# Cross-attention steps of a two-layer attention kernel: value products moved ahead of the next transposes, normalising moved ahead of the probabilities' split

## The reference, cut to what matters

```python
def attention(x, ctx, Wq, Wk, Wv, Wo, bo):
    q = (x @ Wq).reshape(b, n, HEADS, D_HEAD)
    k = (ctx @ Wk).reshape(b, m, HEADS, D_HEAD)
    v = (ctx @ Wv).reshape(b, m, HEADS, D_HEAD)
    sim = jnp.einsum('bihd,bjhd->bhij', q, k) * SCALE
    attn = jax.nn.softmax(sim, axis=-1)
    out = jnp.einsum('bhij,bjhd->bihd', attn, v).reshape(b, n, HEADS * D_HEAD)
    return out @ Wo + bo
h = layernorm(x, ln2_g, ln2_b)
x = attention(h, context, a2_Wq, a2_Wk, a2_Wv, a2_Wo, a2_bo) + x
```

## Time and profile before

| | before |
|---|---|
| median of 3 runs | 1027.96 us (1027.17 to 1029.55) |
| profiled execution, its time | 1026.68 us |
| its span | 1024.9 us |
| TensorE busy | 981.0 us, 96% |
| VectorE busy | 704.5 us, 69% |
| ScalarE busy | 624.1 us, 61% |
| GpSimd busy | 366.3 us, 36% |
| mean granted TensorE clock | 0.981 of 2.4 GHz |
| self-attention, by the trace | about 160 to 565 us |
| cross-attention | about 565 to 877 us |
| feed-forward | about 877 us to the end |

### The profile page before, as it was taken

One profiled execution on the slowest core, in us unless ns is written; L12 is line 12 of the kernel. 1 busy time (PEld: TensorE's weight loads), 2 busy tenths in 40 slices (PEclk: granted clock), 3 DMA queues, 4 the chain that ended last, 5 costly groups with the idle time before them and its releaser, 6 DMA issues.

```text
span 1024.9 us, 21429 instructions
## 1 busy us (share of the span) xinstructions
PE 981.0 (96%) x7892; PEld 921.9 (90%) x7892; DVE 704.5 (69%) x1594; ACT 624.1 (61%) x1945; POOL 366.3 (36%) x514
## 2 busy tenths in 40 slices
PE   7799999999999999999999999999999997999998
PEld 6687877899999999999999989999999997999998
DVE  5577578767676767676778777667667667566674
ACT  5556457757575756565667676676666667433343
POOL 1222337433333333342423345455454545301010
PEclk9799899999999999999999989999999999999999
DMA  7311100104000000000003000200000001001010
GB/s 219 102 42 42 36 21 32 32 2 104 2 22 1 23 1 22 2 21 2 22 2 88 21 27 23 87 27 27 2 27 26 2 22 62 22 22 38 26 32 22
DMA packets 30445, 34.62 MB, mean 34 GB/s; under 512 B 4360, under 2 KB 23816, under 8 KB 30344
## 3 DMA queue, kind: packets, MB, share of 16 engines
q1 hardware_dynamic: 30344, 33.26, 10.7%
HBM read 24.86 MB, written 8.39 MB: 32 GB/s over the span
## 4 chain that ended last, share of the span: by engine, by line
PE 81%; DVE 8%; ACT 7%; issue 2%; POOL 1%; SPq 0%; DMA 0%; DVEq 0%; ACTq 0%
PE bank L1386 15%; PE bank L1388 14%; PE bank L1387 14%; PE bank L1647 8%; PE bank L1626 5%; PE bank L1403 5%; PE bank L1689 3%; PE bank L1691 3%; PE bank L1690 3%; PE bank L1663 3%; ACT p L769 2%; PE bank L1508 1%; PE bank L1509 1%; PE bank L1510 1%; DVE hT_lo L1142 1%
## 5 line engine op out<-in xcount | busy, mean ns | idle before, releaser
L577 POOL TENSOR_TENSOR oT_hi<-oT,ones 128x256 fp32r<-128x256 f32 x128 | 93.9, 733 | 362.7 <-DVE oT L1182 362.7
L769 ACT ACTIVATE p<-bank,negmax 128x256 f32<-128x256 f32 (+1 forms) x512 | 207.8, 427 | 20.2 <-DVE negmax L1159 15.9
L779 ACT CAST pT_hi<-bank 128x512 fp32r<-128x512 f32 (+1 forms) x256 | 110.7, 486 | 166.6 <-PE bank L1647 166.4
L1386 PE MATMUL bank<-hT_hi,w_hi 128*128 128x256 f32 x640 | 188.5, 295 | 3.9 <-DVE qkT_lo L1213 1.6
L1388 PE MATMUL bank<-hT_hi,w_lo 128*128 128x256 f32 x640 | 179.0, 280 | 0.0
L1387 PE MATMUL bank<-hT_lo,w_hi 128*128 128x256 f32 x640 | 178.9, 280 | 0.0
L1174 DVE TENSOR_TENSOR pT_lo<-bank,pT_hi 128x512 fp32r<-128x512 f32 (+1 forms) x256 | 129.6, 547 | 0.5
L1155 DVE TENSOR_REDUCE negmax<-bank 128x2 f32<-128x512 f32 x128 | 82.1, 683 | 66.9 <-PE bank L1626 66.9
L1386 PEld LDWEIGHTS bank<-hT_hi,w_hi 128*128 128x128 f32 x640 | 121.6, 190 | 7.0 <-issue 3.6
L1387 PEld LDWEIGHTS bank<-hT_lo,w_hi 128*128 128x128 f32 x640 | 121.4, 190 | 0.0
L1388 PEld LDWEIGHTS bank<-hT_hi,w_lo 128*128 128x128 f32 x640 | 121.0, 189 | 0.0
(11 more groups left out here) (204 smaller groups left out, 2738.9 us busy)
## 6 DMA issues: line engine op xcount, KB each, us to landing
w_stage<-in_weights SPq DMA_DIRECT2D x47, 256.0 KB, 4.6
x_in<-x_dram SPq DMA_DIRECT2D x24, 256.0 KB, 2.9
x_dram<-x_out SPq DMA_DIRECT2D x16, 256.0 KB, 3.2
l_x<-in_x SPq DMA_DIRECT2D x4, 512.0 KB, 5.0
x_dram<-l_out SPq DMA_DIRECT2D x4, 512.0 KB, 2.8
out_dram<-x_out SPq DMA_DIRECT2D x8, 256.0 KB, 3.1
w_stage<-in_weights SPq DMA_DIRECT2D x9, 128.0 KB, 5.6
l_ctx<-in_ctx SPq DMA_DIRECT2D x4, 180.0 KB, 4.4
```

The source lines that it names most:

```text
L577: nc.gpsimd.tensor_tensor(oh[:, G % PAIRS, :], of[:, :], ones[:, :], ALU.mult).then_inc(y["o_hi"], 1)
L769: last = nc.scalar.activation(p[:, G % 2, e, t * cols:(t + 1) * cols], scores_at(G, e, t), ACT.Exp, bias=negmax[:, G % 2, t, e:e + 1], acc ...
L779: nc.scalar.copy(pTh[0:r, G % 2, e, 0:n], bank[4 + e][0:r, 0:n]).then_inc(y["pT_hi"], 1)
L1386: nc.tensor.matmul(dst, lh, rh, start=(i == 0), stop=False)
```

## The change

In the 64 steps of the cross-attention stage, and only there, three instructions or groups of instructions change their place within the step. TensorE issues the value products of the pair before right behind the scores of the next pair, ahead of this pair's transposes. ScalarE copies that pair's transposed sums ahead of rounding this pair's transposed probabilities. VectorE normalises that pair's output ahead of this pair's low part. What each instruction computes, its operands and its semaphores stay as they are.

```diff
@@ step_cross, ScalarE
                     round_values(b + 1, 0)
+                copy_rT(G - 1)
                 round_pT(G)
                 if G + 1 < STEPS:
                     softmax_pair(G + 1)
...
                     weights_hi(act, 17 + i)
-                copy_rT(G - 1)
@@ step_cross, VectorE
                     values_low(b + 1, 0)
+                normalise_o(G - 1)
                 pT_low(G)
                 if i == 0:
                     prepare_stats(b + 1)
...
                     weights_lo(dve, 17 + i)
-                normalise_o(G - 1)
@@ step_cross, TensorE
                 if G + 1 < STEPS:
                     scores(G + 1)
+                weighted_values(G - 1)
                 transpose_p(G)
...
                 if i in (5, 6) and more:
                     project_queries(b + 1, i - 5)
-                weighted_values(G - 1)
                 if i == 0:
                     project_out(b - 1, 3 if b == B else 5, 6)
```

## The result

The changed kernel takes 1040.62 us (median; 1039.53 to 1041.24) where the kernel before takes 1027.62 us. The ratio is 1.0122, 95% interval 1.0104 to 1.0139: slower by 13 us, as forecast. The profiled span went from 1024.9 to 1037.7 us, +12.8 us.

What follows compares the result with a forecast made beforehand. TensorE was taken as the bound, busy 343 of the stage's 360 us. Terms 3.7 + 0.6 - 2.0 + 10.4 = +12.7 us on 1026.7 give 1039.4; with 1.3 to the median, forecast 1040.5 us, range 1029 to 1051.

Steps and rivals of the forecast that it cites:

- part d: Step 4: key products (line 1403) wait for VectorE's context_low (line 1148) seven times, about 1.8 us, 3 in batch 8.
- The shift per ordinary batch: Key products start 0.61 us later in each ordinary batch, bounds 0.18 and 1.00; six batches give +3.7 us.
- nothing gives the 0.61 us back: After step 4's key products no further wait, order and distances as before, so the 0.61 us delay stays.
- `hT_lo`'s step of 0.82 us: On VectorE, from hT_lo to v_lo: 0.82 us, bounds 0.61 and 1.03, where it took 1.03 us before.
- 747.85 is 747.30 plus the operation's own time: Old trace, by the skill's exclusion rule: hT_lo ends its own duration after GpSimd's x_plus_bias ended.
- part g: TensorE's clock falls after the new 2.0 us idle time in four of six batches, 2.6 us each: +10.4 us.
- Batches 8 and 15: Batch 8, same chain with one weight unit: +0.6 us; batch 15, value products sooner: -2.0 us (bounds -2.9 and -1.2).
- Rival 1: TensorE's clock holds after the new idle time; only +2.3 us remain, 1030.3 us; chance 0.18.
- Rival 2: Clock falls in all six ordinary batches, as long as in batch 8: 20.4 us instead of 10.4, 1050.5 us; chance 0.12.
- Rival 3: context_low doesn't take the wait over, if step 3's chain moves by less than 0.75 us: 1015 us; chance 0.12.
- (c): VectorE's normalise_o ahead of pT_low: in step 3 it runs in idle time, taking 0.33 us off the chain.
- (a): TensorE's value products ahead of the transposes: free for TensorE, but dependent ScalarE and VectorE work starts 0.93 us later.

Runs made afterwards that it cites:

- after_late_lows: Changed kernel with VectorE's prepare_lo and values_low moved from step 3 to step 4, behind context_low: 1018.55 us, ratio 0.9899.
- old_in_34: Changed kernel with the old order on all three engines in steps 3 and 4 of each batch: 1024.51 us, ratio 0.9974.
- after_busy: Changed kernel with twelve transposes of the identity added on TensorE in step 4, behind pair 4's transposes: 1025.70 us, ratio 0.9968.
- late_all: after_late_lows with ScalarE's prepare and round_values also in step 4 and VectorE's weight-unit low parts one step later: 1008.53 us, ratio 0.981.
- before_late_all: Kernel before, without the change's three moves, with all the later moves of late_all: 1008.79 us, ratio 0.9812.
- pe_only: Kernel before with TensorE's move alone; ScalarE and VectorE keep their old order: 1083.87 us, ratio 1.054.
- norm_late: Changed kernel with VectorE's normalise_o put back at the end of its step: 1085.32 us, ratio 1.0552.
- no_pe_move: Changed kernel with TensorE's move taken back, ScalarE's and VectorE's moves kept: 1135.92 us, ratio 1.1059.

## Why the prediction was right, point by point

**The new wait** (what is late next, part d). Right: line 1403 on VectorE's line 1148, seven times, 1.65 to 1.68 us in ordinary batches (forecast about 1.8) and 2.93 in batch 8 (forecast 3). Its cause is shown by `after_late_lows`, its place by `old_in_34`.

**The shift per ordinary batch** was mis-sized: 0.33 us by `after_busy`, where I had 0.61 (within the bounds 0.18 and 1.00). Two things are at fault. `copy_rT` was costed at 0.22 us ahead of the rounding; the rounding moved by 0.98 us, of which 0.93 are the value products, so the copy costs 0.05: it runs beside the transposes and is nearly hidden by them. And "nothing gives the 0.61 us back" was not quite true: the key products come 0.42 us later against the context transposes, but a batch is only 0.33 longer. The other 0.1 us comes back somewhere in the six other steps; I haven't pinned it down, but it is of the size of the 0.15 us by which `late_all`'s ordinary batches are shorter than `before_late_all`'s, where neither has a wait. `hT_lo`'s step of 0.82 us was right (757.30 less 756.50, 0.80). The reading that 747.85 is 747.30 plus the operation's own time was off: the sum is 747.99.

**The clock** (part g) had the right mechanism and price per fall and too few of them. I took four falls of 2.6 us. There were six. From batch 9 to batch 14 the key products moved from 640.07 to 837.87, 197.8 us for five batches, against 185.0 in `after_busy`: 12.8 us for five falls, 2.6 each. With the sixth, a short one of 1.7, it is 14.5 us instead of 10.4. Against that stands the shift of 0.33 instead of 0.61 (2.0 us instead of 3.7). So the total for the six batches, 16.5 us, is 2.4 us above my 14.1.

**Batches 8 and 15.** From batch 8's key products to batch 14's, six batches, the distance grew by 14.8 us: 238.0 us (837.87 less 599.85) against 223.2 before (823.28 less 600.07). That is less than 16.5 since it ends ahead of the sixth fall. The rest of the span's +12.8 lies on both sides. The stage began 1.2 us sooner in the changed kernel (the wait on `qkT_lo` ends at 565.42, where it was 566.64), in a part that has no edit, and batch 8's key products came 0.2 us sooner: batch 8 cost 1.0 (forecast 0.6). From batch 14's key products to the first feed-forward product 1.5 us were won (62.1 us, before 63.7) although the sixth fall is there, and 0.3 us behind it, where nothing was edited: batch 15 gave some 3.2 us, more than my 2.0 and my bound of 2.9. Its waits on `oT` went from 6.0 to 3.9 us, and its clock fell once where it had fallen twice. That the sum came out within 0.2 us of the median is partly these errors cancelling: the six batches cost 2.4 us and batch 8 0.4 us more than forecast, batch 15 gave 1.2 us more, and 1.5 us came from parts without an edit. The signs, the places and the largest term held, the single sizes less. The last step of the sum was also 0.2 us off (1039.4 and 1.3 make 1040.7).

**Rival 1** (the clock holds) fell with the six falls. The Trainium skill ("TensorE: Matmul & The Clock Gate", "HAM oscillation — how this bites in real kernels") ties a fall to idle gaps longer than any in this stage; the trace disagrees, with falls after 1.65 to 1.68 us. The +2.3 us that the rival would have left was too much as well. `after_busy` tells it: against the kernel before, batch 8's chain cost 1.0 us there and the ordinary batches 2.0, and from batch 14's key products to the first feed-forward product 3.1 us were won (60.6 us, before 63.7), which leaves about nothing; batch 8's shorter fall, worth 1.7, then turns the total below the kernel before. **Rival 2** (all six, all long) was half right: all six, three long. **Rival 3** (faster) fell at the point that I had named: the chain moved by 0.98 us, above 0.75.

**What I had not seen** is the loop of `pe_only`. I costed (c) as 0.33 us of one chain, though it is a condition for (a): without it the kernel takes 45 us more.

## What to carry to other kernels

When a wait is to be removed by reordering, look at what is queued behind it on the same engine and who wants that: here TensorE would have waited for two things that came within 0.1 us of each other, and taking away the first made the second longer. The cure was at the head of the chain (two operations of another step that nobody needed yet, queued ahead of the one that TensorE wanted), not at its end. And an idle time has two prices, its length and what it does to TensorE's clock afterwards; where it can't be avoided, harmless work that fills it can be worth more than the idle time itself (here 15 us, for six waits of 1.7 and one of 2.9 us).

## What the runs showed of the hardware that I had not expected

The length of an idle time alone doesn't say whether the clock falls. In the changed kernel 1.65 to 1.68 us were enough in six of six batches, with the key products of 120 columns next. In `pe_only` TensorE was idle for 2.10 us in step 4 of each of the batches 9 to 14, with value products of 256 columns next, and in the eight microseconds behind it the clock held in batches 10, 11 and 12 and fell in 9, 13 and 14:

```profile
697.27 0.41 PE L1663 MATMUL bank<-ident,rsum_wide 128*128 128x128 f32 x2 [2.10 <-DVE oT L1182]
...
651.30:659.30 8.00, 8.00 (x42) 8.00 (x42) 2.66 (x8) 3.49 (x13) 4.00 (x6) 0.56 0.94 306
697.30:705.30 8.00, 8.00 (x67) 7.80 (x68) 4.83 (x12) 5.76 (x25) 3.98 (x6) 1.00 0.14 43
738.70:746.70 8.00, 7.96 (x66) 7.83 (x67) 4.89 (x12) 5.69 (x24) 4.04 (x6) 1.00 0.14 43
780.20:788.20 8.00, 8.00 (x67) 7.80 (x68) 4.85 (x12) 5.73 (x24) 4.01 (x6) 1.00 0.15 48
821.70:829.70 8.00, 8.00 (x43) 8.00 (x44) 2.89 (x9) 3.50 (x13) 3.98 (x6) 0.57 0.13 41
866.54:874.54 8.00, 8.00 (x41) 8.00 (x42) 2.50 (x8) 3.49 (x13) 3.98 (x6) 0.55 0.08 25
```

The order of the instructions is the same in these six batches and so is the wait. So neither the length nor the kind of work on either side settles it alone; `norm_late` has the like, 2.16 us in six batches with a fall in two of them. Ahead of the key products the count is one-sided: `no_pe_move` waited 1.58 or 1.59 us there in batches 9 to 14, and the clock fell in all six as in the changed kernel. No run varies that neighbour with the rest held, so it stays a pattern, and what decides stays open. A forecast of a fall should therefore be given as a chance and a price, as was done here, and not as a threshold.
